# Layer 0 of a graph network: edge attributes laid out as the product's operand before they are loaded

## The reference

```python
K = (x @ Wk).reshape(n, H, DH)
q_dst = Q[dst] + rel_q[edge_type].reshape(-1, H, DH)
k_src = K[src] + rel_k[edge_type].reshape(-1, H, DH)
k_src = k_src + (time_emb @ Wt + bt).reshape(-1, H, DH)      # time_emb is edge_attr_32: (103125, 32)
euclid = jnp.sum(q_dst * k_src, axis=-1) / np.float32(np.sqrt(DH))
decay = jnp.exp(decay_scale * jnp.tanh(relu(dec_in @ Wd1 + bd1) @ Wd2 + bd2))
hyp = -hyp_beta * man_dist * decay        # man_dist = |m[src] - m[dst]|
logits = alpha * (euclid * decay) + (1.0 - alpha) * hyp
# then a softmax over the edges of each target node, a weighted sum of v_src, and a feed-forward part
```

## Time and profile before

| | |
|---|---|
| median of 3 runs | 4768.07 us (4766.82 to 4777.56) |
| profiled execution | 4801.0 us, span 4799.2 us |
| granted TensorE clock, mean | 0.807 |
| busy over the span | PE 3465.4, DVE 3315.7, ACT 2163.7, POOL 1895.9 us |
| layer 0's loop | from about 190 to 1940 us of the span |

### The profile page before, as it was taken

One profiled execution on the slowest core, in us unless ns is written; L12 is line 12 of the kernel. 1 busy time (PEld: TensorE's weight loads), 2 busy tenths in 40 slices (PEclk: granted clock), 3 DMA queues, 4 the chain that ended last, 5 costly groups with the idle time before them and its releaser, 6 DMA issues.

```text
span 4799.2 us, 86810 instructions
## 1 busy us (share of the span) xinstructions
PE 3465.4 (72%) x31241; PEld 2866.3 (60%) x31241; DVE 3315.7 (69%) x6625; ACT 2163.7 (45%) x6244; POOL 1895.9 (40%) x2178
## 2 busy tenths in 40 slices
PE   1377777776777777353666467886969999959996
PEld 1255544444555555233666457875569999959995
DVE  5466655555555555447999688786776666679997
ACT  2355544444555555134888455665022222224443
POOL 0355566654555555400000031000035555538884
PEclk7676777776767777576778778998989999979998
DMA  4555545555555554201000022011524444413332
GB/s 111 176 153 151 154 138 148 141 145 127 148 151 155 154 152 138 60 0 39 11 13 10 13 86 80 37 44 42 173 87 125 124 129 124 123 40 126 131 126 72
DMA packets 458227, 498.47 MB, mean 104 GB/s; under 512 B 179661, under 2 KB 397839, under 8 KB 457656
## 3 DMA queue, kind: packets, MB, share of 16 engines
q1 hardware_dynamic: 403639, 328.47, 23.8%
q0 software_dynamic: 54144, 164.25, 11.7%
HBM read 381.72 MB, written 110.84 MB: 103 GB/s over the span
## 4 chain that ended last, share of the span: by engine, by line
PE 36%; DVE 22%; POOL 15%; issue 14%; ACT 7%; DMA 3%; SPq 2%; another core or an unknown queue 1%; POOLq 0%; ACTq 0%; DVEq 0%
POOL arena_a L1178 12%; PE psum L3687 4%; PE psum L3703 3%; PE psum L3638 3%; PE psum L3636 3%; POOL arena_c L1216 3%; PE psum L2990 2%; PE psum L3603 2%; ACT arena_c L2953 2%; PE psum L3662 2%; DVE arena_a L3183 2%; PE psum L3685 2%; PE psum L3275 1%; PE psum L3634 1%; DVE arena_c L3176 1%
## 5 line engine op out<-in xcount | busy, mean ns | idle before, releaser
L1178 POOL DMA_INDIRECT arena_a<-src_table,src_tix x808 | 822.7, 1018 | 428.8 <-issue 386.3
L3407 POOL TENSOR_SCALAR node_hot<-arena_c 128x128 fp32r<-128x128 f32 x575 | 369.2, 653 | 900.5 <-DVE arena_c L3295 567.8
L3425 DVE SCALAR_TENSOR_TENSOR msg_parts<-psum,msg_parts 128x512 fp32r<-128x512 f32 (+2 forms) x644 | 425.2, 660 | 260.0 <-ACT msg_parts L3574 228.2
L3125 POOL TENSOR_SCALAR node_hot_dst<-arena_c 128x128 fp32r<-128x128 f32 x587 | 383.7, 670 | 122.5 <-DVE arena_c L3529 67.9
L3574 ACT ACTIVATE msg_parts<-psum 128x512 fp32r<-128x512 f32 (+2 forms) x325 | 186.5, 574 | 520.4 <-PE psum L3638 520.4
L2990 PE MATMUL psum<-arena_a,arena_c 128*128 128x150 f32 x1800 | 287.7, 329 | 175.4 <-ACT arena_c L2956 175.4
L3636 PE MATMUL psum<-arena_c,arena_a 128*128 128x128 bf16 x3675 | 406.4, 220 | 0.0
L3638 PE MATMUL psum<-arena_c,arena_a 128*128 128x128 bf16 x3675 | 406.4, 220 | 0.0
L2990 PEld LDWEIGHTS psum<-arena_a,arena_c 128*128 128x128 f32 x1800 | 282.1, 224 | 178.5 <-ACT arena_c L2956 178.5
L2429 PE MATMUL psum<-win_parts,pick_w 128*128 128x256 f32 x1616 | 388.3, 392 | 0.0
L1856 DVE TENSOR_TENSOR arena_a<-arena_a,psum 128x512 f32<-128x512 f32 x202 | 138.0, 683 | 346.6 <-issue 222.8
(11 more groups left out here) (585 smaller groups left out, 10323.2 us busy)
## 6 DMA issues: line engine op xcount, KB each, us to landing
y_rows<-arena_c SPq DMA_DIRECT2D x101, 576.0 KB
arena_a<-bucket_rows SPq DMA_DIRECT2D x150, 384.0 KB
arena_a<-bucket_rows SPq DMA_DIRECT2D x50, 448.0 KB
arena_a<-bucket_lists SPq DMA_DIRECT2D x25, 896.0 KB
pair_counts<-arena_c SPq DMA_DIRECT2D x25, 800.0 KB
arena_a<-bucket_lists SPq DMA_DIRECT2D x25, 704.0 KB
arena_a<-src_table,src_tix POOLq DMA_INDIRECT x808
arena_c<-edge_attr SPq DMA_DIRECT2D x100, 128.0 KB
```

Source lines behind the costliest of these rows:

```text
L1178: e.indirect_dma_start(out_, None, table, bass.IndirectOffsetOnAxis(ap=idx, axis=0)).then_inc(sem, 16)
L3125: return e.tensor_scalar(node_hot3[at % RING_H][:, i, :], iota_row, dst_lo[:, b, t:t + 1], None, ALU.is_equal)
L3407: return e.tensor_scalar(node_hot[at % RING_M][:, i, :], iota_row, src_lo[:, b, 2 * k + j:2 * k + j + 1], None, ALU.is_equal)
L3425: e.scalar_tensor_tensor(out=to[:, 1, 0:nt, :], in0=bank[at % 4][:, 0:nt * P].rearrange("p (t f) -> p t f", f=P), scalar=0.0, in1=to[:, 0, ...
```

## The change

`kernel()` writes `edge_attr_32` into a padded array in which each block is a 128 x 2 x 128 piece: partition = 32 x (tile within the half) + attribute, then half, then edge within the tile. It does no arithmetic. Each block is then one load of 128 rows of 1024 bytes straight into one of four `eat` buffers (`RING_EA`). The two `ea` buffers, the two transposes, ScalarE's copy, their semaphores and the two memsets go. PE's wait for the loads stays where it was; its wait for the previous block's tanh, which frees bank 3, moves from ahead of the transposes to just ahead of L2459. SP's wait for `ea_turned` goes, and one for the product of four blocks earlier stands ahead of the attribute load.

```diff
+RING_EA = 4
...
-        ea = [c_.take(TPB * T_DIM).rearrange("p (t f) -> p t f", t=TPB) for _ in range(2)]
-        eat = [c_.take(2 * P).rearrange("p (t f) -> p t f", t=2) for _ in range(2)]
+        eat = [c_.take(2 * P).rearrange("p (t f) -> p t f", t=2) for _ in range(RING_EA)]
...
                 e.wait_ge(g.hid_pe, (1 if stacked else 2) * (k - 1))
-                e.wait_ge(g.ea_turned, k - 1)
...
-            t0 = k * TPB
-            ea_view = a["edge_attr_32"]
-            if k < NBLK - 1:
-                e.dma_start(ea[s][:, :, :], ea_view[t0 * P:(t0 + TPB) * P, :].rearrange("(t p) c -> p t c", p=P)).then_inc(g.d_rows[s], 16)
-            else:
-                ...
+            if k >= RING_EA:
+                e.wait_ge(g.addend_pe, 2 * (k - RING_EA + 1))
+            e.dma_start(eat[k % RING_EA][:, :, :], a["edge_attr_32"][k]).then_inc(g.d_rows[s], 16)
...
-                if b0:
-                    e.wait_ge(g.ea_turned, i0 + 1)
-                    if i0 >= 2:
-                        e.wait_ge(g.addend_pe, 2 * (i0 - 1))
-                    e.activation(eat[s0][:, :, :], bank[3][:, 0:2 * P].rearrange("p (h f) -> p h f", h=2), ACT.Copy).then_inc(g.eat_ready, 1)
...
-            for s in range(2):
-                e.memset(hid[s][HID:HID + 1, :], 1.0)
-            e.memset(ea[0][:, :, :], 0.0)
-            e.memset(ea[1][:, :, :], 0.0).then_inc(g.l0_prep, 1)
+            e.memset(hid[0][HID:HID + 1, :], 1.0)
+            e.memset(hid[1][HID:HID + 1, :], 1.0).then_inc(g.l0_prep, 1)
...
-            e.wait_ge(g.eat_ready, k + 1)
             if at:
                 e.wait_ge(g.addend_used, at)
-            e.matmul(bank[0][:, :], eat[s][:, hf, :], Wt4[:, :], start=True, stop=True).then_inc(g.addend_pe, 1)
+            e.matmul(bank[0][:, :], eat[k % RING_EA][:, hf, :], Wt4[:, :], start=True, stop=True).then_inc(g.addend_pe, 1)
...
                 if b0:
-                    e.wait_ge(g.d_rows[s0], 48 * turns(i0, 2) + (16 if i0 == NBLK - 1 else 0))
-                    if i0:
-                        e.wait_ge(g.decay_tanh, i0)
-                    for hf in range(2):
-                        turned = e.transpose(bank[3][:, hf * P:(hf + 1) * P], ea[s0][:, 4 * hf:4 * hf + 4, :].rearrange("p t c -> p (t c)"), ident[:, :])
-                    turned.then_inc(g.ea_turned, 1)
+
+                    e.wait_ge(g.d_rows[s0], 48 * turns(i0, 2))
...
                 if b0:
-                    e.wait_ge(g.eat_ready, i0 + 1)
+                    if i0:
+                        e.wait_ge(g.decay_tanh, i0)
                     e.matmul(bank[3][:, :], wd1_2, dec_2[s0], start=True, stop=True).then_inc(g.hid_pe, 1)
...
+def attributes_turned(v):
+
+    full = np.zeros((NBLK * TPB * P, T_DIM), v.dtype)
+    full[0:E] = v
+    return np.ascontiguousarray(full.reshape(NBLK, 2, 4, P, T_DIM).transpose(0, 2, 4, 1, 3)).reshape(NBLK, P, 2, P)
...
+        if name == "edge_attr_32":
+            v = attributes_turned(v)
```

More of the change, by code:

```diff
@@ L183, in __init__ @@
         self.l0_prep = sem("l0_prep")
-        self.ea_turned = sem("ea_turned")
-        self.eat_ready = sem("eat_ready")
+        self.spare = [sem(f"spare{i}") for i in range(2)]
         self.hid_pe = sem("hid_pe")
@@ L290, in of_layer0 @@
                 self.type_dve, self.type_pe, self.stage_pe, self.stage_act, self.stage_dve, self.base_ready,
-                self.windows_ready, self.l0_prep, self.ea_turned, self.eat_ready, self.hid_pe, self.hid_act,
+                self.windows_ready, self.l0_prep, *self.spare, self.hid_pe, self.hid_act,
                 self.q_pe, self.q_used, self.m_pe, self.m_used, self.decay_pe, self.decay_tanh, self.decay_dve,
@@ L913, in sp_l0_loads @@
                 e.dma_start(dec_to, dec_rows[:, (2 * k + hf) * 512:(2 * k + hf + 1) * 512]).then_inc(g.d_rows[s], 16)
-            t0 = k * TPB
-            ea_view = a["edge_attr_32"]
-            if k < NBLK - 1:
-                e.dma_start(ea[s][:, :, :], ea_view[t0 * P:(t0 + TPB) * P, :].rearrange("(t p) c -> p t c", p=P)).then_inc(g.d_rows[s], 16)
-            else:
-                nf = FULL - t0
-                e.dma_start(ea[s][:, 0:nf, :], ea_view[t0 * P:FULL * P, :].rearrange("(t p) c -> p t c", p=P)).then_inc(g.d_rows[s], 16)
-                e.dma_start(ea[s][0:TAIL, nf, :], ea_view[FULL * P:E, :]).then_inc(g.d_rows[s], 16)
+            if k >= RING_EA:
+                e.wait_ge(g.addend_pe, 2 * (k - RING_EA + 1))
+            e.dma_start(eat[k % RING_EA][:, :, :], a["edge_attr_32"][k]).then_inc(g.d_rows[s], 16)
         def sp_load_window_keys(e, k, layers):
@@ L1459, in act_l0_any @@
                 s0, s1, r1 = i0 % 2, i1 % 2, i1 % RING
-                if b0:
-                    e.wait_ge(g.ea_turned, i0 + 1)
-                    if i0 >= 2:
-                        e.wait_ge(g.addend_pe, 2 * (i0 - 1))
-                    e.activation(eat[s0][:, :, :], bank[4][:, 0:2 * P].rearrange("p (h f) -> p h f", h=2), ACT.Copy).then_inc(g.eat_ready, 1)
                 if b1:
@@ L2280, in rows_base @@
         def rows_base(s, layers):
-            return lane_base(s, 2, 1, 48) + (16 if s == (NBLK - 1) % 2 else 0) + lane_base(s, 2, layers - 1, 16)
+            return lane_base(s, 2, 1, 48) + lane_base(s, 2, layers - 1, 16)
         def dve_layer3_tail(e, own):
@@ L2504, in pe_l0_any @@
                 if b0:
-                    e.wait_ge(g.d_rows[s0], 48 * turns(i0, 2) + (16 if i0 == NBLK - 1 else 0))
-                    if i0:
-                        e.wait_ge(g.decay_tanh, i0)
-                    for hf in range(2):
-                        turned = e.transpose(bank[4][:, hf * P:(hf + 1) * P], ea[s0][:, 4 * hf:4 * hf + 4, :].rearrange("p t c -> p (t c)"), ident[:, :])
-                    turned.then_inc(g.ea_turned, 1)
+                    e.wait_ge(g.d_rows[s0], 48 * turns(i0, 2))
                 if b2:
@@ L2525, in pe_l0_any @@
                             e.wait_ge(g.addend_used, 2 * (i0 - 1) + hf + 1)
-                        e.matmul(bank[hf][:, :], eat[s0][:, hf, :], Wt4[:, :], start=True, stop=True).then_inc(g.addend_pe, 1)
+                        e.matmul(bank[hf][:, :], eat[i0 % RING_EA][:, hf, :], Wt4[:, :], start=True, stop=True).then_inc(g.addend_pe, 1)
                 if b3:
```

## The result

The changed kernel takes 4718.92 us (median of 4 runs, 4711.82 to 4721.38), the kernel before 4770.72 us (4 runs, 4766.82 to 4777.56). The ratio is 0.9887, 95% interval 0.987 to 0.9905: 52 us faster.

The account below looks back on a forecast made before the run. It took a ring of waits through POOL's gathers and power to bound layer 0's loop; 101 blocks x 0, plus 2 us at the side job's end and 1.7 us at the start, took 3.7 us off 4768.1: 4764 us, range 4722 to 4780.

Parts of the forecast that it names:

- a ring of waits: Layer 0's loop: gathers, gap, L1830, scores, squares and power set the period, 16.8 us, not one engine's work.
- The step that failed: Layer 0's loop: of PE's 0.33 us saved per block, 0 shortens the period; all of it if that reading is wrong.
- a gift of 1.46 us: Two blocks of the trace: PE's L2459 came 1.46 us earlier in the second, and L1830 gained nothing.
- The transposes: PE, each block: two transposes less save 0.22 us, at most 0.4 us at the low clock; counted 0 for the period.
- The hand-over: L2459 no longer waits for ACT's copy: counted with the transposes, 0.3 us; ACT's 0.39 us copy itself worth 0.
- The attribute load: DMA, each block: larger rows relieve the engines by 0 to 1.5 us; counted 0, since no engine waits for transfers.
- The end of the side job: About 1100 us, SP's queue: 896 descriptors fewer bring store L904 forward 0 to 3.8 us; taken as 2 us.
- The start: Start of layer 0's loop: two memsets and the time from first transpose to L2459 go, 1.7 us saved.
- PE's time on the ring after all: Rival: L1830 moves with L2459 by 0.33 us a block, 33 us faster, 4731 us (4724 to 4742); chance 0.20.
- The traffic rival: Lighter DMA traffic brings the gathers' landing forward 0.3 us a block: 30 us faster, 4734 us; chance 0.18.
- the clock rival: Less PE work keeps PE at 1.2 GHz; iterations without DVE's wait pay 1.9 us: 27 us slower, 4791 us; chance 0.12.
- What would show it: Signs in the next profile: right with powers 16.8 us apart; wrong and slower with granted clock well under 0.72.

Follow-up runs that it names:

- e1c: The changed kernel with two transposes that nobody reads put back on PE in the old place: 4762.7 us, 0.9978 of before (4770.9 us).
- e10c: The kernel before with only the first pair of sums moved behind the second half's products: 4715.2 us, 0.9828 of before (4797.5 us).
- e3c: The kernel before with only its attribute load in rows of 1024 bytes: 4777.8 us, 1.0009 of before (4770.9 us).
- e7: The changed kernel with four transposes that nobody reads put on PE in the old place: 4783.8 us, 1.002 of before (4774.0 us).
- e5: The changed kernel measured again without any edit: 4721.7 us, 0.9896 of before (4771.8 us).
- e1: The changed kernel with two transposes that nobody reads put back on PE: 4456.7 us, 0.9987 of before (4459.9 us).
- e3: The kernel before with only its attribute load in rows of 1024 bytes: 4455.9 us, 0.9993 of before (4459.9 us).
- e4: The changed kernel with its attributes loaded in rows of 128 bytes: 4456.4 us, 0.9987 of before (4459.9 us).

## Why the prediction was wrong

**What bounds the kernel.** That no engine fills the loop, that a ring of waits sets the period, and which ring it is, was right for before: eight gathers, a gap, L1830, scores, squares, power. So was the reading that L1830 follows the gathers and not the row of L2459. From 1200 to 1840 us the start of this row moves between 8.1 and 6.5 us ahead of the power, while L1830 stays 3.28 us ahead of it and 1.48 us behind the last gather. The earlier trace rows fit too: with the ninth gather POOL's part is 13.7 to 13.8 us in place of 12.0, 1.7 of the 2.1 us. The two operations that DVE does more there (L1806, L1807) hold nothing up: it waits again behind them. What was wrong is the next step, from "L1830 does not follow PE's row" to "nothing done to PE's time can matter".

**The step that failed** reads: "Of it, on the ring: 0 by the earlier trace rows, since L1830 ignored a gift of 1.46 us. If that reading is wrong, all of it." Two transposes cost 41 us (e1c), moved sums are worth 82 us in before (e10c). PE's time does not move the moment at which the held signals come out, and in so far L1830 ignores it; but it decides which signals are still held, and so how many of DVE's instructions stand behind that moment: 3.28 us of work to the power when it is the keys, 2.68 or 2.08 us when it is the products of the second half. I had taken the place of the wait as fixed, and POOL's 4.76 us with it; they fell to 3.85. The earlier trace rows could not show this, since both of its blocks wait at the keys. Its gift was not one either.
```profile
1422.38 1.51 PE L2428 MATMUL psum<-win_parts,pick_w 128*128 128x256 f32 x8
...
1423.23 0.30 DVE L1896 TENSOR_TENSOR arena_c<-arena_c 64x128 f32<-64x128 f32 x1
1423.46 0.67 DVE L1829 TENSOR_TENSOR arena_c<-psum,dst_col 128x512 f32<-128x512 f32 x1
...
1426.91 0.69 DVE L1857 TENSOR_TENSOR arena_a<-arena_a,psum 128x512 f32<-128x512 f32 x1 [2.18 <-remote]
1426.97 0.69 ACT L1358 ACTIVATE arena_c<-psum 128x272 f32<-128x272 f32 x2 [2.79 <-remote]
```

The keys' signal was out in time here: L1829 does not wait. The row of L2428, the last product of this half, ends at 1422.38 + 1.51 = 1423.89; L1857 on DVE, which waits for it, begins at 1426.91, and ACT's eviction of later sums at 1426.97. By the semaphore times five signals of PE come out between 1426.89 and 1427.08 us, for rows that ended between 1423.89 and 1425.40, and right behind them, from 1427.08 to 1427.53, 16 landing signals of the gathers, after a pause of 0.94 us. In the block of the earlier trace rows it is five signals from 1532.65 to 1532.88 for rows from 1528.85 to 1531.54. Work that takes 1.5 or 2.7 us by its rows is not done in 0.2 us, so the signals were held and let go together; PE itself need not have been late. Perfetto Trace Analysis, Tensor Engine Instruction, of the Trainium skill says that this engine's end is estimated from the instruction's size, and that the signal follows the acknowledged write to PSUM; the trace agrees as far as the order goes, and only the runs gave the 3 us.

**The other terms.** The transposes: sized 0.22 to 0.4 us, measured 0.40 as a cost over all blocks. That the two agree is luck: the cost is a share of blocks times a step of 0.6 us, not PE's time. The hand-over: inside my 0.33 us, measured 0.13 by itself, with ACT's copy in it. 41 + 13 = 54 us, and the change gives 50 to 52, so these two account for it, though costs that come in steps need not add up. The attribute load 0: right (e3c). The moved wait for tanh and SP's new wait 0: no wait for either shows in after. The end of the side job, 2 us: three powers there take 1149.70 - 1082.18 = 67.5 us in before, 17.2 more than three blocks, and 1114.70 - 1050.81 = 63.9 us in after, 16.7 more; 0.5 us by one trace of each. The start, 1.7 us: 1.1 us.

**The rivals.** The first, PE's time on the ring after all, comes nearest: 4731 us forecast, 4724 to 4742 by its bounds, 4719 measured. It had 0.20, and its mechanism was half right: L1830 does not move with L2459 by 0.33 us a block, it stops being the instruction that waits, and the time falls in steps. The traffic rival is out by e3c, the clock rival by the windows: 0.75, not lower. TensorE: Matmul & The Clock Gate, Part 4, of the Trainium skill says that transposes don't count for that clock. e1c neither shows nor refutes it: with the two transposes back the granted clock is 0.75 from 1200 to 1840 us, as in after, but from 200 to 600 us it is 0.76, and 0.77 with four (e7), where after has 0.73 and e5, the same kernel, 0.74.

**What would show it.** "Wrong, and faster: powers 16.5 us apart or less and a shorter wait of POOL": both came, 15.73 and 3.85 us. The last sentence of the forecast, that it fails if the hold on PE's signal depends on PE's own instructions, comes close to what happened: not the end of the hold depends on them, but what it catches.

**Left open.** Why PE's signals come out 3 us and more behind its rows; why they do so where before takes 4771 us and not where it takes 4460; and what decides, block by block, which signal is caught: the rows don't tell, for the keys' row ended 2.1 us ahead of the last gather's end in the block of the earlier trace rows and was held, and 1.7 us ahead in the block of after and was not. That the hold ends with the gathers is read from the traces, by its constant distance in nine kernels and by the earlier trace rows; no run moved or removed a gather in the steady part.

## What to carry to other kernels

When a consumer stands although the rows of a matmul have ended, don't look for the cause in those rows: a row's end is a model, and the consumer's start is a measurement. Measure instead from what else happens at a constant distance, here the last gather. Then count what stands behind the late signal: a wait costs as much as the work that has to follow it, so ask which instruction waits, and not only how long. Work that nobody in the next half block needs (here a pair of sums, 0.45 us) belongs behind the awaited products; that one move was worth as much as removing transposes, copy and hand-over. And a trace in which all blocks wait at one place cannot show what happens when the wait moves, so a term of "0 because it didn't follow" needs a run.

## What the runs showed of the hardware

The same kernel before took 4771 to 4798 us in some sets of runs and 4460 to 4467 us in others, 7% apart, with medians within 0.6% inside a kind, all of it in one loop of four. The same chip showed both, 4467 us and later 4797 us, so it is not the chip alone. The granted clock from 200 to 600 us was 0.82 in the faster kind (e1, e3, e4) and 0.73 in the slower (before, after), and yet it is no sufficient cause: e10c, of the slower kind, had 0.82 from 1200 to 1840 us and powers 15.68 us apart, where e3 had 0.81 and 13.69. In e3 PE's signals kept up with its rows, and no comparison of keys waited. In e10c they were held, 3.0 us in the block shown, and five were let go within 0.2 us. In the nine kernels of the slower kind the held signal came, in the mean, 1.2 to 1.5 us behind the last of POOL's gathers. A change that is worth 1.1% in one kind moved close relatives of it by 0.1% in the other, and moving the sums in before was worth 1.0% and 1.7%. A verdict on such a loop holds for the kind in which it was taken.
